# A graph layer on one core: TensorE's order inside a tile step

## Chip, core and metric

The kernel runs on one NeuronCore of a Trainium2 chip. The metric is the device time of one execution in microseconds; the kernel before was timed three times, with a median of 1980.95 us.

## What is computed

The input is x, 6250 nodes by 256 features, and 106250 edges (src, dst) that are sorted by dst, with two weights each. Cut to what matters:

```
xn  = layernorm(x)
low  = relu(segment_sum(edge_weight    * (xn @ W_low)[src],  dst))
high = relu(segment_sum(edge_weight_n2 * (xn @ W_high)[src], dst))
mlp  = relu(xn @ W_mlp)
att  = softmax(sigmoid([low@a_l, high@a_h, mlp@a_m]) @ att_vec / 3)
x1   = x + 3 * (att0*low + att1*high + att2*mlp) + mix(xn)
x2   = layernorm(x1)
w    = x2 @ wr + br
y    = gelu(x2 @ w1 + b1) @ w2 + b2        # FFN, 256 -> 1024 -> 256
out  = x1 + x2 + (y * w for the 3124 nodes with the largest w, else 0)
```

`mix` is a linear attention with an MLP over all nodes. The kernel multiplies by W_low and W_high after the sum over edges, which is the same.

## The kernel before

**First stage** (about 830 us of the profiled span). The nodes are handled in tiles of 128 rows, 49 in all. The edges are sorted by destination into 98 buckets of 64 nodes; the sorted records go to HBM by 448 indirect scatters on GpSimd (L648). Layer norm, `mix` and the third branch run beside it. None of it is touched.

**Second stage, the tile steps.** `pipeline` calls a function `stage(i, here, before1, before2, before3)` for i = 0 to 49 on each engine; the code is unrolled, every engine has its own list and they meet by semaphores alone. The flags say which tiles are in flight: in step i, `here` sums the edges of tile i, `before1` does the weight products of tile i-1, `before2` the FFN's first product of tile i-2, `before3` the FFN's second product of tile i-3.

The work of a step, by engine:

- **GpSimd** (L665) gathers the columns: one indirect DMA fetches 128 rows of xn (one edge on each partition) into a ring of 32 columns, 852 columns in all, about 8.7 a bucket. It waits for `col_free` ahead of each group of 8. **SyncE** (L554 to L564) watches gathers land in fours (`g_ready`) and hands columns back in groups of 8, when `sel_used` says that TensorE has used them; it does both in one queue, in order.
- **VectorE**: `post_b(i-2)` (L1203 to L1209: x2, its row sum with wr), `bucket(2i)`, `post_a(i-1)`, `bucket(2i+1)`. A `bucket` builds the one-hot weights of 2 x 5 columns (L1116 makes the mask, L1122 multiplies by the edge weights), signalled by `sel_ready`. `post_a` (L1164 to L1197) waits for `lh_ready`, makes two logit sums (L1167), exchanges two tanh with ScalarE, and forms x1 and the start of a Newton iteration.
- **TensorE** (matmuls at L1528, transposes at L1817 and L1827): a bucket is 10 products of 128 x 256 in fp32, accumulated in PSUM (bank 0 for the first bucket of a tile, bank 1 for the second). A step is: transposes of the two summed buckets (`before1`), bias row, transposes of x2, **weight products** (4), **first bucket**, `down` (8 products: FFN out), `up` (16 products of 128 x 128: FFN in), **second bucket**. An fp32 product is two matmul instructions in the profile.
- **ScalarE**: `sums(i)` copies the second bucket (L1443), the transposed sums (L1447), and makes the Relu copy of the weight products (L1452, `lh_ready`); `copy_x2t` (L1456); the copy of the first bucket (L1490, waits for `sel_used` 4i+2); `attention` (two tanh, L1460 and L1462); `newton` (L1468 to L1473); `scale_y` (L1481); the GELUs (L1438).

A bucket on TensorE waits twice for columns and twice for select weights:

```
pe.wait_ge(S("g_ready"), pe.snap(lo + VIS))
pe.wait_ge(S("sel_ready"), 2 * b + 1)
...
pe.wait_ge(S("g_ready"), pe.snap(rest + BOTH))
pe.wait_ge(S("sel_ready"), 2 * b + 2)
```

Once per step a chain crosses three engines: first bucket done, its copy and a tanh on ScalarE, `post_a` on VectorE, then VectorE's select of the second bucket, then TensorE's second bucket.

Of the kernel before, what the change touches and what calls it, by code (L numbers as in the profile page):

```python
# [43 lines left out]
def wait(eng, sem, value):  # L44

    if isinstance(value, int) and value <= 0:
        return
    eng.wait_ge(sem, value)


def build(nc, a, out):
# [47 lines left out]
    with ExitStack() as ctx:  # L99
        sems = {}  # L100

        def S(name):
            if name not in sems:
                sems[name] = ctx.enter_context(nc.semaphore(name))
            return sems[name]
# [121 lines left out]
        here = r2.take([P, NBUF, VIS, BK], BF16)  # L227
# [136 lines left out]
        bank = [ctx.enter_context(nc.psum_tensor(f"bank{i}", [P, 512], F32)) for i in range(8)]  # L364
# [39 lines left out]
        def bucket_word(eng, b):  # L404

            return eng.value_load(packed[0:1, b:b + 1], min_val=0, max_val=2 ** (2 * CBITS) - 1)

        def first_col(eng, word):
            return eng.snap(word % 2 ** CBITS, min_val=0, max_val=COLS - 1)

        def extra_cols(eng, word):
            return eng.snap((word // 2 ** CBITS) % 2 ** CBITS, min_val=0, max_val=COLS - 1)
# [883 lines left out]
        def _(act):  # L1296
# [138 lines left out]
            def gelu(i, part):  # L1435
                act.wait_ge(S("f1_psum"), 2 * i + part + 1)
                for f in range(part * KF // 2, (part + 1) * KF // 2):
                    act.activation(fh[:, f, :], bank[4 + part][:, (f % 4) * P:(f % 4 + 1) * P], ACT.Gelu_apprx_tanh,  # L1438
                                   bias=b1f[:, f:f + 1]).then_inc(S("fh_ready"), 1)

            def sums(i):
                act.wait_ge(S("sel_used"), 4 * i)
                act.activation(agg[:, 1, :], bank[1][:, 0:D], ACT.Copy).then_inc(S("agg_b"), 1)  # L1443
                act.wait_ge(S("at_psum"), i)

                for k in range(KD):
                    ins = act.activation(aggt[:, k, :, :].rearrange("p v (h n) -> p v h n", h=2),  # L1447
                                         bank[2][:, k * D:(k + 1) * D].rearrange("p (h v n) -> p v h n", h=2, v=2), ACT.Copy)
                ins.then_inc(S("aggt_ready"), 1)
                act.wait_ge(S("lh_psum"), i)  # L1450
                wait(act, S("lh_used"), i - 1)
                act.activation(lh[:, :], bank[3][:, :], ACT.Relu).then_inc(S("lh_ready"), 1)  # L1452

            def copy_x2t(a):
                act.wait_ge(S("xt_psum"), a + 1)
                act.activation(x2t[:, :, :].rearrange("p k n -> p (k n)"), bank[6][:, 0:D], ACT.Copy).then_inc(S("x2t_ready"), 1)  # L1456

            def attention(i):
                act.wait_ge(S("lg_ready"), i)
                act.activation(sg[:, 0, :], lg[:, :], ACT.Tanh, scale=0.5).then_inc(S("sig_tanh"), 1)  # L1460
                act.wait_ge(S("att_in"), i)
                act.activation(sg[:, 6, :], sg[:, 3, :], ACT.Tanh, bias=sg[:, 5, 0:1], scale=-1.0).then_inc(S("att_tanh"), 1)  # L1462
# [15 lines left out]
            def scale_y(a):  # L1478
                act.wait_ge(S("y_psum"), a + 1)
                act.wait_ge(S("w_ready"), a + 1)  # L1480
                act.activation(side[:, ds(a * D, D)], bank[7][:, 0:D], ACT.Copy, scale=wall[:, ds(a, 1)]).then_inc(S("y_ready"), 1)  # L1481

            def stage(i, here, before1, before2, before3):
                if before1:
                    sums(i)
                if before2:
                    copy_x2t(i - 2)
                if here:
                    act.wait_ge(S("sel_used"), 4 * i + 2)
                    act.activation(agg[:, 0, :], bank[0][:, 0:D], ACT.Copy).then_inc(S("agg_a"), 1)  # L1490
                if before1:
                    attention(i)
                if not here:

                    scale_y(i - 3)
                    gelu(i - 2, 0)
                    newton(i)
                    gelu(i - 2, 1)
                    return
                if before1:  # L1500
                    newton(i)
                if before3:
                    scale_y(i - 3)
                if before2:
                    gelu(i - 2, 0)
                    gelu(i - 2, 1)
# [19 lines left out]
        def _(pe):  # L1526
# [243 lines left out]
            def add_col(acc, weights, col, start, stop):  # L1770

                at = pe.snap((col % GR) * D)
                return mm(acc[:, 0:D], weights, rows[:, ds(at, D)], start, stop, skip_group_check=True)

            def bucket(b, acc):

                word = bucket_word(pe, b)
                lo = first_col(pe, word)
                more = extra_cols(pe, word)
                pe.wait_ge(S("g_ready"), pe.snap(lo + VIS))  # L1780
                pe.wait_ge(S("sel_ready"), 2 * b + 1)
                for j in range(VIS):
                    ins = add_col(acc, msel[:, 2 * b % NBUF, j, :], lo + j, j == 0, False)
                ins.then_inc(S("sel_used"), 1)
                with pe.If(more > 0):
                    done = extras_so_far(pe, b)
                    with pe.Fori(0, more) as e:
                        pe.wait_ge(S("g_ready"), pe.snap(lo + e + VIS + 1))
                        pe.wait_ge(S("sel_x_ready"), pe.snap(done + e + 1))
                        add_col(acc, msel_x[:, :], lo + e + VIS, False, False).then_inc(S("sel_x_used"), 1)  # L1790
                rest = pe.snap(lo + more)
                pe.wait_ge(S("g_ready"), pe.snap(rest + BOTH))
                pe.wait_ge(S("sel_ready"), 2 * b + 2)
                for j in range(VIS):
                    ins = add_col(acc, msel[:, (2 * b + 1) % NBUF, j, :], rest + VIS + j, False, j == VIS - 1)
                ins.then_inc(S("sel_used"), 1)
# [15 lines left out]
            def stage(i, here, before1, before2, before3):  # L1812
                if before1:
                    pe.wait_ge(S("agg_b"), i)
                    for k in range(KD):
                        for h in range(2):
                            ins = pe.transpose(bank[2][:, k * D + h * P:k * D + (h + 1) * P], agg[:, h, k * P:(k + 1) * P], ident[:, :])  # L1817
                    ins.then_inc(S("at_psum"), 1)
                if before3:

                    wait(pe, S("y_ready"), i - 3)
                    mm(bank[7][:, 0:D], ones_b[0:65, :], b2f3[0:65, :], True, False)
                    pe.wait_ge(S("fh_ready"), (i - 2) * KF)
                if before2:
                    pe.wait_ge(S("x2_ready"), i - 1)
                    for k in range(KD):
                        ins = pe.transpose(bank[6][:, k * P:(k + 1) * P], x2n[:, k * P:(k + 1) * P], ident[:, :])  # L1827
                    ins.then_inc(S("xt_psum"), 1)
                if before1:
                    if isinstance(i, int) and i == 1:  # L1830
                        pe.wait_ge(S("gnn_loaded"), 16 * 2)
                    pe.wait_ge(S("aggt_ready"), i)
                    wait(pe, S("lh_ready"), i - 1)
                    for v, w in enumerate((wlow, whigh)):
                        for k in range(KD):
                            ins = mm(bank[3][:, v * D:(v + 1) * D], aggt[:, k, v, :], w[:, k, :], k == 0, k == KD - 1)
                    ins.then_inc(S("lh_psum"), 1)
                if here:
                    wait(pe, S("agg_a"), i)
                    bucket(2 * i, bank[0])  # L1840
                if before3:
                    down(0, KF).then_inc(S("y_psum"), 1)
                if before2:
                    if isinstance(i, int) and i == 2:
                        pe.wait_ge(S("ffn_loaded"), 16 * 2)
                    pe.wait_ge(S("x2t_ready"), i - 1)
                    for part in range(2):
                        up(part).then_inc(S("f1_psum"), 1)
                if here:
                    wait(pe, S("agg_b"), i)  # L1850
                    bucket(2 * i + 1, bank[1])
# [64 lines left out]
```

## Time and profile before

| | us |
|---|---|
| timed, median of 3 runs | 1980.95 |
| timed, lowest and highest | 1979.86, 1987.71 |
| the profiled execution, its span (first to last instruction) | 2481.7 |
| TensorE matmuls busy | 1719.4 (69%) |
| GpSimd busy | 1371.7 (55%) |
| VectorE busy | 1229.1 (50%) |
| ScalarE busy | 924.8 (37%) |

The profile is of one execution, and for it only the span is given. It is 501 us longer than the median of the timed runs, so its parts can't be added up to the timed value without asking which of them belong to the profiled execution alone. PE is TensorE, PEld its weight loads, DVE VectorE, ACT ScalarE, POOL GpSimd, SP SyncE. In a row of a timeline the first number is the start, the second the length in us, then engine, line, operation, output<-input and count; the bracket holds the idle time before it and what ended it. "issue" is idle time for which the profile shows no wait.

### The profile page before, as it was taken

What the parts mean: (1) busy time and instruction counts of PE and PEld (TensorE: products, weight loads), DVE (VectorE), ACT (ScalarE), POOL (GpSimd) and SP (SyncE); (2) the same over time, 40 slices, a digit from 0 to 9 for tenths busy, and PEclk for the clock granted to TensorE, in tenths of its full rate; (3) what the DMA queues carried; (4) which work ended last, traced back from release to release, by engine and by line L of the source; (5) the groups of instructions that cost most, each with busy time, mean ns of one, the idle gap of its engine ahead of it and who ended that gap; (6) DMA issues with size and microseconds to landing.
All of it is one profiled execution on the core that took longest, in us unless ns stands there. A gap on an engine that the chain in (4) does not pass through costs nothing.

```text
span 2481.7 us, 30518 instructions
## 1 busy us (share of the span) xinstructions
PE 1719.4 (69%) x9109; PEld 1441.9 (58%) x9109; DVE 1229.1 (50%) x3164; ACT 924.8 (37%) x2641; POOL 1371.7 (55%) x1351
## 2 busy tenths in 40 slices
PE   4788884998865347776777677677577677667672
PEld 4566673887754335665665666566466566556562
DVE  8899995888761223432343333333333333333336
ACT  2677873777652112321222222222222222222223
POOL 3277675788776565545555455455455545554600
PEclk9899996999967667888887888788788788788886
DMA  3221211111100422222222222222222222222303
GB/s 90 72 63 54 80 33 30 46 54 46 46 5 5 133 85 72 78 69 75 71 74 71 68 73 75 65 72 75 68 73 75 75 69 71 81 71 68 85 9 104
DMA packets 102212, 162.99 MB, mean 66 GB/s; under 512 B 32190, under 2 KB 72762, under 8 KB 102040
## 3 DMA queue, kind: packets, MB, share of 16 engines
q0 software_dynamic: 55232, 113.59, 16.4%
q1 hardware_dynamic: 46808, 47.29, 6.0%
q8 instruction: 85, 1.39, 0.2%
q14 instruction: 87, 0.71, 0.1%
HBM read 139.76 MB, written 21.04 MB: 65 GB/s over the span
## 4 chain that ended last, share of the span: by engine, by line
PE 51%; issue 23%; DVE 10%; ACT 9%; another core or an unknown queue 5%; DMA 1%; SPq 1%; POOL 0%; DVEq 0%; ACTq 0%; POOLq 0%
PE bank L1528 49%; ACT side L1303 2%; PE bank L1817 1%; ACT base L1303 1%; ACT arena L1303 1%; DVE arena L811 1%; ACT arena L1447 1%; ACT arena L1443 1%; DVE arena L733 1%; ACT side L1519 1%; DVE arena L766 1%; ACT arena L1307 0%; PE bank L1602 0%; DVE arena L781 0%
## 5 line engine op out<-in xcount | busy, mean ns | idle before, releaser
L1528 PE MATMUL bank<-arena 128*128 128x128 f32 (+3 forms) x6320 | 1292.5, 359 | 508.2 <-issue 426.8
L1528 PEld LDWEIGHTS bank<-arena 128*128 128x128 f32 (+1 forms) x6320 | 1094.8, 205 | 683.8 <-issue 500.0
L665 POOL DMA_INDIRECT arena<-xn_rows,arena x852 | 825.5, 969 | 733.8 <-SPq L564 450.0
L648 POOL DMA_INDIRECT sorted_records<-arena x448 | 523.0, 1167 | 256.0 <-issue 139.3
L1167 DVE CUSTOM_DVE_ANT_0 arena<-arena 128x256 f32<-128x256 f32 x98 | 37.8, 423 | 414.9 <-ACT arena L1452 376.1
L1122 DVE TENSOR_TENSOR arena<-arena 128x640 f32<-128x640 bf16 (+1 forms) x204 | 164.2, 805 | 47.6 <-DVE arena L1116 17.7
L1172 DVE SCALAR_TENSOR_TENSOR att_prod<-sg,att_neg 128x9 f32<-128x9 f32 x49 | 8.5, 174 | 334.9 <-issue 300.8
L1490 ACT ACTIVATE arena<-bank 128x256 f32<-128x256 f32 x49 | 18.8, 383 | 355.5 <-remote 262.1
L1116 DVE SCALAR_TENSOR_TENSOR arena<-io,arena 128x320 bf16<-128x320 f32 (+1 forms) x204 | 97.8, 479 | 106.3 <-DVE wall L1209 43.5
L1528 PE MATMUL bank<-arena,base 128*128 128x128 f32 (+3 forms) x766 | 118.4, 287 | 16.7 <-ACT base L1307 8.3
L1438 ACT ACTIVATE arena<-bank,b1f 128x128 f32<-128x128 f32 x392 | 110.3, 372 | 33.5 <-PE bank L1528 28.1
L811 DVE TENSOR_TENSOR arena<-arena 128x1280 f32<-128x1280 bf16 x84 | 120.5, 1488 | 4.1 <-remote 1.7
L1528 PEld LDWEIGHTS bank<-arena,base 128*128 128x128 f32 (+2 forms) x766 | 110.2, 211 | 17.6 <-ACT base L1307 8.5
L1443 ACT ACTIVATE arena<-bank 128x256 f32<-128x256 f32 x49 | 18.8, 383 | 247.0 <-PE bank L1528 219.3
L1528 PE MATMUL bank<-side,arena 128*128 128x512 f32 x196 | 97.1, 619 | 0.3 <-issue 0.3
L1481 ACT ACTIVATE side<-bank,wall 128x256 f32<-128x256 f32 x49 | 23.1, 472 | 176.0 <-remote 165.3
L1303 ACT ACTIVATE base<-arena 128x128 f32<-128x128 f32 x280 | 84.7, 391 | 9.4 <-DVE arena L792 9.4
L1468 ACT ACTIVATE nr<-nri 128x1 f32<-128x1 f32 x49 | 9.9, 203 | 206.0 <-issue 159.8
L1303 ACT ACTIVATE arena<-arena 128x128 f32<-128x128 f32 x280 | 84.6, 397 | 0.0
L1303 ACT ACTIVATE side<-arena 128x128 f32<-128x128 f32 x280 | 84.6, 392 | 0.0
L1528 PE MATMUL bank<-arena,side 128*128 128x128 f32 x560 | 73.5, 282 | 12.0 <-issue 10.9
L1528 PEld LDWEIGHTS bank<-arena,side 128*128 128x128 f32 x560 | 68.0, 196 | 15.6 <-issue 14.1
(312 smaller groups left out, 1889.2 us busy)
## 6 DMA issues: line engine op xcount, KB each, us to landing
arena<-xn_rows,arena POOLq DMA_INDIRECT x852
sorted_records<-arena POOLq DMA_INDIRECT x448
arena<-in_x SPq DMA_DIRECT2D x12, 512.0 KB
xn_rows<-arena SPq DMA_DIRECT2D x12, 512.0 KB
x_plus_xn_rows<-arena SPq DMA_DIRECT2D x12, 512.0 KB
arena<-x_plus_xn_rows SPq DMA_DIRECT2D x12, 512.0 KB
arena<-xn_rows SPq DMA_DIRECT2D x12, 512.0 KB
out<-base SPq DMA_DIRECT2D x4, 1024.0 KB
```

Source lines behind the costliest of these rows:

```text
L648: pool.indirect_dma_start(rec_dram, bass.IndirectOffsetOnAxis(ap=idx[0:PR, par, u:u + 1], axis=0), stage_rec[0:PR, par, u * 8:(u + 1) * 8] ...
L665: pool.indirect_dma_start(gring[:, c % GR, :], None, xn_dram, bass.IndirectOffsetOnAxis(ap=rring[:, c, 3:4].bitcast(I32), axis=0)).then_in ...
L733: ins = dve.tensor_tensor(oh[:, t, :].rearrange("p j (h e) -> p j h e", e=2), twice[:, t, :].unsqueeze(2).to_broadcast([P, GS, NB // 2, 2] ...
L766: dve.tensor_tensor(prod4[:, :, :, 0:NB], oh[:, :, :].rearrange("p (s j) b -> p s j b", s=GROUPS), rankf[:, :].rearrange("p (s b) -> p s b ...
L811: dve.tensor_tensor(cellrec[:, t, :].rearrange("p t (f c) -> p t f c", f=4), cell[:, t, :].unsqueeze(2).to_broadcast([P, GS, 4, GC]), raw[ ...
L1116: return dve.scalar_tensor_tensor(out_, io64[:, :].unsqueeze(1).to_broadcast([P, n, BK]), float(BK * b), r[:, :, 0:1].to_broadcast([P, n, ...
L1122: return dve.tensor_tensor(out_, hots.unsqueeze(2).to_broadcast([P, n, 2, BK]), r[:, :, 1:3].unsqueeze(3).to_broadcast([P, n, 2, BK]), ALU ...
L1167: ins = dve.tensor_tensor_reduce(out=lg_prod[:, k, :], in0=lh[:, k * D:(k + 1) * D], in1=att_rows[:, k, :], scale=1.0, scalar=0.0, op0=ALU ...
L1303: ins = act.activation(quot[:, j, :], iota32[:, :], ACT.Abs, bias=p32[:, par, s * GS + j:s * GS + j + 1], scale=-1.0)
L1438: act.activation(fh[:, f, :], bank[4 + part][:, (f % 4) * P:(f % 4 + 1) * P], ACT.Gelu_apprx_tanh, bias=b1f[:, f:f + 1]).then_inc(S("fh_re ...
L1443: act.activation(agg[:, 1, :], bank[1][:, 0:D], ACT.Copy).then_inc(S("agg_b"), 1)
L1528: return pe.matmul(out_, lhsT, rhs, start=start, stop=stop, **kw)
```

## The change

TensorE runs the first bucket of a tile ahead of the weight products of the tile before, not behind them. ScalarE's Relu copy of those products moves from the end of `sums` to just ahead of `attention`, so that its copies keep TensorE's order: second bucket, transposed sums, x2, first bucket, Relu. The waits and semaphore counts are the same, and no instruction is added or taken away. In the last step (i = 49), where there is no bucket, ScalarE makes the x2 copy ahead of the Relu.

```
@@ scalar: sums(i)
                 ins.then_inc(S("aggt_ready"), 1)
+
+            def low_high(i):
                 act.wait_ge(S("lh_psum"), i)
                 wait(act, S("lh_used"), i - 1)
                 act.activation(lh[:, :], bank[3][:, :], ACT.Relu).then_inc(S("lh_ready"), 1)
@@ scalar: stage
                 if before1:
+                    low_high(i)
                     attention(i)
@@ tensor: stage
+                if here:
+                    wait(pe, S("agg_a"), i)
+                    bucket(2 * i, bank[0])
                 if before1:
...
                     ins.then_inc(S("lh_psum"), 1)
-                if here:
-                    wait(pe, S("agg_a"), i)
-                    bucket(2 * i, bank[0])
                 if before3:
                     down(0, KF).then_inc(S("y_psum"), 1)
```

## Rows read from the trace of the kernel before

**Rows 1.** The page: busy time of each engine, and the granted TensorE clock by slice.

```profile
PE 1719.4 (69%) x9109; PEld 1441.9 (58%) x9109; DVE 1229.1 (50%) x3164; ACT 924.8 (37%) x2641; POOL 1371.7 (55%) x1351
...
PEclk9899996999967667888887888788788788788886
```

**Rows 2.** Busy time by stretch of the span (start:end, length, then each engine).

```profile
core 0: us, PE busy (x) PEld busy (x) DVE busy (x) ACT busy (x) POOL busy (x), PEclk, DMA share, GB/s
...
832.00:2373.00 1541.00, 1059.66 (x4864) 897.34 (x4865) 542.86 (x1758) 378.46 (x1230) 825.19 (x852) 0.82 0.26 75
2373.00:2482.00 109.00, 50.66 (x245) 39.46 (x243) 59.13 (x158) 35.23 (x102) 0.19 (x1) 0.73 0.18 60
```

**Rows 3.** The list of waits, whole span: us in total, times, longest.

```profile
PE bank L1528 <- issue: 454.7, 347, 9.2
...
POOL arena L665 <- SPq L564: 450.0, 67, 13.1
```

**Rows 4.** One step in order of time, 1520 to 1528 us: TensorE and ScalarE.

```profile
1520.85 0.30 PE L1528 MATMUL bank<-arena 128*128 128x128 f32 x1 [1.83 <-issue]
...
1523.66 0.37 PE L1528 MATMUL bank<-arena 128*128 128x128 f32 x1 [2.52 <-issue]
...
1527.36 0.47 ACT L1481 ACTIVATE side<-bank,wall 128x256 f32<-128x256 f32 x1 [4.29 <-remote]
```

**Rows 5.** Stretches inside two steps; the number behind POOL's is the granted clock.

```profile
2368.70:2382.00 13.30, 13.30 (x76) 11.99 (x76) 5.43 (x25) 2.92 (x10) 2.98 (x4) 1.00 0.15 41
...
1521.00:1527.00 6.00, 0.89 (x3) 0.86 (x3) 3.46 (x8) 1.88 (x7) 3.10 (x3) 0.50 0.30 87
```

**Rows 6.** The last full step in order of time: ScalarE, TensorE and VectorE.

```profile
2366.85 0.38 ACT L1443 ACTIVATE arena<-bank 128x256 f32<-128x256 f32 x1 [4.83 <-PE bank L1528]
...
2367.89 0.38 PE L1827 MATMUL bank<-ident,arena 128*128 128x128 f32 x2
...
2368.69 13.34 PE L1528 MATMUL bank<-arena 128*128 128x256 f32 x76 [0.42 <-ACT arena L1447]
...
2370.72 0.60 ACT L1452 ACTIVATE arena<-bank 128x512 f32<-128x512 f32 x1 [2.08 <-PE bank L1528]
...
2371.35 0.43 DVE L1167 CUSTOM_DVE_ANT_0 arena<-arena 128x256 f32<-128x256 f32 x1 [9.04 <-ACT arena L1452]
...
2375.04 0.38 ACT L1490 ACTIVATE arena<-bank 128x256 f32<-128x256 f32 x1 [3.44 <-PE bank L1528]
...
2375.32 0.20 ACT L1460 ACTIVATE sg<-lg 128x3 f32<-128x3 f32 x1
...
2381.25 0.49 DVE L1116 SCALAR_TENSOR_TENSOR arena<-io,arena 128x320 bf16<-128x320 f32 x1 [0.69 <-issue]
...
2381.89 0.82 DVE L1122 TENSOR_TENSOR arena<-arena 128x640 f32<-128x640 bf16 x1
...
2383.02 2.20 PE L1528 MATMUL bank<-arena 128*128 x9 [1.00 <-DVE arena L1122]
```

**Rows 7.** GpSimd in order of time, where nothing holds it.

```profile
1507.20 0.95 POOL L665 DMA_INDIRECT arena<-xn_rows,arena  x1 [0.31 <-issue]
1508.45 0.95 POOL L665 DMA_INDIRECT arena<-xn_rows,arena  x1 [0.30 <-issue]
```

**Rows 8.** The page: GpSimd's gathers in groups.

```profile
L665 POOL DMA_INDIRECT arena<-xn_rows,arena x852 | 825.5, 969 | 733.8 <-SPq L564 450.0
```

**Rows 9.** ScalarE in order of time, 790 us: a stall ahead of the tile steps.

```profile
789.89 0.60 ACT L1326 ACTIVATE arena<-bank 128x512 f32<-128x512 f32 x1 [28.11 <-remote]
```

**Rows 10.** After the last step, in order of time: logit sums to tanh.

```profile
2409.57 0.43 DVE L1167 CUSTOM_DVE_ANT_0 arena<-arena 128x256 f32<-128x256 f32 x1 [7.91 <-ACT arena L1452]
...
2410.39 0.20 ACT L1460 ACTIVATE sg<-lg 128x3 f32<-128x3 f32 x1 [0.57 <-DVE lg L1167]
```

**Rows 11.** VectorE in order of time: `post_b` of a tile.

```profile
2400.02 0.41 DVE L1203 TENSOR_SCALAR arena<-arena,mv,nr 128x256 f32<-128x256 f32 x1
...
2401.26 0.21 DVE L1209 TENSOR_SCALAR wall<-nr,br 128x1 f32<-128x1 f32 x1
```

More of the change, by code:

```diff
@@ L1449, in sums, with low_high @@
                 ins.then_inc(S("aggt_ready"), 1)
+            def low_high(i):
                 act.wait_ge(S("lh_psum"), i)
@@ L1491, in stage @@
                 if before1:
+                    low_high(i)
                     attention(i)
@@ L1828, in stage @@
                     ins.then_inc(S("xt_psum"), 1)
+                if here:
+                    wait(pe, S("agg_a"), i)
+                    bucket(2 * i, bank[0])
                 if before1:
@@ L1837, in stage @@
                     ins.then_inc(S("lh_psum"), 1)
-                if here:
-                    wait(pe, S("agg_a"), i)
-                    bucket(2 * i, bank[0])
                 if before3:
```

## Prediction

> **What bounds the kernel now.** I read the totals first, then the stretches, then the list of waits, then single steps in order of time. The totals say TensorE 69% and GpSimd 55% [rows 1]; the stretches say that 1541 of the 2481.7 us lie between the first and the last of 852 column gathers on GpSimd, with TensorE busy for 1059.66 us of them [rows 2]. That is the stage of the 49 tile steps, and the only place where the diff does anything.
>
> The profiled execution is no picture of the timed one: 2481.7 us of span against a median of 1980.95, so 501 us are extra. The waits show where: TensorE idles 454.7 us for nothing that the profile names, in 347 pieces [rows 3]. In one step they look like this: single matmuls about 2.1 us apart, while ScalarE waits for a "remote" release [rows 4]. The granted clock is 0.50 there (the 1.2 GHz level) and 1.00 (2.4 GHz) in a step without such gaps [rows 5]. GpSimd's 450.0 us of waiting for SyncE's column credits [rows 3] are the same stalls seen from the producer: TensorE is late, the ring of 32 columns is full. I take these stalls as belonging to the profiled execution, because only their removal brings the span near the timed runs, and I cost the change on steps without them.
>
> The cleanest step is the last full one. Its 76 matmul instructions run in one piece of 13.34 us [rows 6], and the number fits: 8 for the weight products, 20 for the first bucket, 16 for the FFN's second product (`down`), 32 for its first (`up`). Counted from ScalarE's copy of the second bucket at 2366.85:
> - weight products start at 2368.69, 1.84 us later;
> - they are done at 2370.72 (the Relu copy starts), the first bucket at 2375.04 (its copy starts), 4.32 us later;
> - TensorE is through `down` and `up` at 2368.69 + 13.34 = 2382.03;
> - the second bucket starts only at 2383.02, after 1.00 us of waiting for VectorE's selection weights.
>
> So the way from "first bucket done" to "second bucket starts" is not TensorE's 7.0 us but 8.0 us through ScalarE's copy and tanh (2375.32), VectorE's attention work, and the select (2381.25 and 2381.89) [rows 6]. From a bucket's first matmul to its copy: 6.35 us for 28 instructions less 8 x 0.216 us (4.32 / 20), 4.62. The next step's origin is 2387.64; one step is 20.8 us, 49 are 1019.
>
> GpSimd has its own step. Gathers start 1.25 us apart when nothing holds them [rows 7], with 0.30 us idle between; by the group's mean of 969 ns [rows 8] plus 0.30 it is 1.27. 852 / 49 = 17.4 columns a step: 21.7 to 22.1 us, 1065 to 1082 in all. That is above 20.8. Which of the two holds in the timed runs? Take the profiled span, remove the gather stretch (1541) and one named stall of 28.1 us before it [rows 9], and 912.6 are left. The median leaves 1981 - 913 = 1068 us for the stage, 21.8 a step. GpSimd's pace gives 1065 to 1082, TensorE's chain 1019. So I hold that the timed kernel is bound by GpSimd's gather pace, with about 1 us a step of slack behind it. What lies outside the span isn't shown, nor are the smaller stalls of the first stage; they pull in opposite directions, so the fit is good to perhaps 30 us.
>
> On GpSimd's spans the Trainium skill (Perfetto Trace Analysis, section GPSIMD Engine Instruction) advises timing by start-to-start spacing and not by the reported duration. The trace agrees that the two differ, 1.25 against 0.969; by the duration alone the stage would be 852 x 0.969 = 826 us and TensorE's chain would bound instead.
>
> **The change part by part.** No instruction is added or removed; matmuls, copies, semaphores and waits are the same.
> - First bucket moved ahead of the weight products. Before, TensorE idles 0.42 us for ScalarE's transposed copy ahead of the weights [rows 6]. After, it can go on right behind the transposes of the FFN input, which end at 2367.89 + 0.38 = 2368.27 and are followed at issue pace: bucket at about 2368.2 instead of weights at 2368.69. Gain in TensorE's own order: 0.49 us a step. What it could meet instead is its own select (below) or its columns; where the gathers bind, waiting for columns at this place costs nothing, since the gathers run on.
> - Weight products moved behind the bucket. The Relu copy starts 6.35 us after the bucket's first matmul (28 instructions, the same count as now): 2374.55 instead of 2370.72.
> - ScalarE: copy of the first bucket at about 2372.82 instead of 2375.04, then the wait for the weights, then Relu, then the tanh. Queued behind that new wait are tanh, Newton steps, `scale_y` and the GELUs. VectorE waits for the Relu before the logit sums: before, these were long done while the bucket ran; now they are in the chain. From the Relu's start to VectorE 0.63 (2370.72 to 2371.35) [rows 6], from there to the tanh 0.82 (2409.57 to 2410.39) [rows 10]: tanh at 2376.00 instead of 2375.32, **0.68 us later**, although the bucket ended 2.2 earlier. Everything behind the tanh keeps its length, so the second bucket starts at 2383.70. TensorE is through with `up` at 2368.2 + 13.34 = 2381.54 and waits 2.2 us instead of 1.0.
> - GELUs of `up`: ScalarE's Newton steps follow VectorE's guess, so they slide by the same 0.68 and are read by `down` a step later, more than 10 us on: nothing.
> - SyncE's queue: it frees columns after each half bucket. Credits of the first bucket come 2.2 us earlier, those of the second 0.7 later. Worst case a full group of 8 columns (10 us) late once; best case nothing. The ring holds 32 columns and a bucket reads 10, so with GpSimd as the bound GpSimd never waits for it; nothing.
> - VectorE's select of the next first bucket is needed earlier: at 2387.64 + 0.68 + 1.35 = 2389.7 (the bucket starts 2368.20 - 2366.85 = 1.35 us into a step) instead of 3.6 us into it. By the rows: the second select's other half takes 1.4 us behind 2383.4 (one half is 1.46 us, 2381.25 to 2382.71) [rows 6], `post_b` 1.45 us (2400.02 to 2401.47) [rows 11], the next half select 0.7 + 1.46: 2388.4. It fits with 1.3 us; if it did not, what it is late would come on top.
>
> Sum for a step: chain 20.8 + 0.7 = 21.5 us, against GpSimd's 21.7 to 22.1. The later chain is still covered, by 0.2 to 0.6 us. What is uncovered is the end: once the last columns have landed, first bucket to second bucket takes 2383.70 - 2372.82 = 10.9 us instead of 8.0. That is +2.9 us, once. Forecast 1981 + 3 = **1984 us**.
>
> **The rivals.**
> - *Gathers don't bind, the chain does* (slower). The logit sums come into the chain from tanh to select; 49 x 0.68 = +33 us: 2014, or about half of it, 1998, where GpSimd binds in some steps and the chain in others. It decides as soon as the gathers' pace is below 21.5 us a step, that is below 1.235 us a column; 1.25 is only 1% above it. For it: 0.2 us of cover is thin, buckets differ in width, and the stage of 1068 us is known to 30. Against: 1019 is 49 us too short for the stage of before.
> - *TensorE's own order binds* (faster). If `down` and `up` (7.0 us at clock 1.00) take longer than the new chain from Relu to select, 2383.70 - 2374.55 = 9.15 us, the chain is hidden and 49 x 0.49 = 24 us come back: 1957. This needs a mean granted clock under 7.0 / 9.15 = 0.77 in that piece; the stretch had 0.82, but with the stalls in it [rows 2], and 1.00 in the clean step [rows 5].
> - *Nothing is reached*: each step's weights wait anyway for something else. That is the forecast's own time.
>
> The Trainium skill (Perfetto Trace Analysis, section Identifying the Most-Contended Engine) takes the engine with the highest occupancy as the bottleneck. By that rule it is TensorE, 69% against 55%, and the result would be the faster rival's 1957. The row of GpSimd's pace and the stage's length speak against it here.
>
> **How the numbers follow.** Covered by the gathers, 1984: 0.55. Chain, fully or in part, 1998 to 2014: 0.33. TensorE's own order, 1957 to 1971: 0.12. A measurement of this kernel tells about 0.5% (10 us) from no change, so these are also the chances of same, slower and faster. The range takes in the first two cases with 2 us above the full price, and goes down to 1968, which leaves most of the faster case out: 1968 to 2016.
>
> **What would show it.** In the profile of the changed kernel, in a step whose 76 matmuls run in one piece: the bucket's copy (now ahead of the Relu) about 6 us after the second bucket's copy; the Relu 1.7 us behind it; the tanh 1.4 us behind the Relu; TensorE's wait for the select 2.2 us instead of 1.0. Gathers still 1.25 us apart. The profiled span may move by tens of us with the stalls and decides nothing. I am wrong if GpSimd's free-running pace in the timed runs is not that of the profile, or if TensorE's clock without stalls stays low enough that its matmuls set the step.

## The result and the profile after

The changed kernel takes 2023.32 us (median of 4), the kernel before, run beside it, 1982.8: a ratio of 1.0194, 95% interval 1.0178 to 1.0209. It is about 40 us slower, outside the forecast's range by 7 us, and not the "no change" that I held likeliest.

The profiled execution of the changed kernel spans 2024.8 us; nothing of the 2.1 us gaps of [rows 4] is in it. The page of after:

```profile
span 2024.8 us, 30518 instructions
PE 1611.9 (80%) x9109; PEld 1364.5 (67%) x9109; DVE 1226.6 (61%) x3164; ACT 920.7 (45%) x2641; POOL 1388.0 (69%) x1351
...
PEclk9899999699999776899999999999999999999975
```

A second profile of the kernel before (the first experiment) spans 1979.9 us, as long as its timed runs. It, and not the one in front, is what after has to be held against. Its page:

```profile
span 1979.9 us, 30518 instructions
PE 1569.8 (79%) x9109; PEld 1325.9 (67%) x9109; DVE 1230.2 (62%) x3164; ACT 915.0 (46%) x2641; POOL 1395.7 (70%) x1351
```

Where the 44.9 us between the two spans lie can be read from one row a step, ScalarE's copy of the second bucket (L1443). Before, its first start is at 809.5 and its 49th at 1902.7, 1093.2 us apart; after, at 812.1 and 1946.7, 1134.6 apart. So 41.4 us of the 44.9 arise in the tile steps: 32 in the 45 steps of the middle, 5 in the two ahead of them, 4 in the last one (41.7 us instead of 37.9). Over 830 to 1880 us the granted clock is 0.94, against 0.98 in the second profile of before; in the page's tenths both look like 9. The waits of TensorE and GpSimd in the tile steps (830 to 1880 us), of after:

```profile
PE bank L1531 <- DVE arena L1122: 113.2, 55, 9.2
...
POOL arena L665 <- SPq L564: 42.9, 42, 3.5
...
PE bank L1531 <- SPq L554: 0.2, 1, 0.2
```

and of the second profile of before:

```profile
PE bank L1528 <- DVE arena L1122: 51.2, 46, 4.5
PE bank L1528 <- SPq L554: 47.4, 24, 4.9
...
POOL arena L665 <- SPq L564: 21.0, 69, 0.3
```

The bound has changed hands. Before, TensorE waits 47.4 us for landed columns (SyncE's L554) and GpSimd never for more than its usual 0.3 us: the gathers set the pace. After, TensorE never waits for columns, GpSimd now waits up to 3.5 us for freed ones, and TensorE's total wait for VectorE's select has more than doubled.

Two neighbouring steps of after in order of time, which answer to [rows 6]:

```profile
1259.01 0.38 ACT L1443 ACTIVATE arena<-bank 128x256 f32<-128x256 f32 x1 [3.41 <-PE bank L1531]
...
1260.66 13.33 PE L1531 MATMUL bank<-arena 128*128 x76 [0.22 <-issue]
...
1265.27 0.38 ACT L1492 ACTIVATE arena<-bank 128x256 f32<-128x256 f32 x1 [4.20 <-PE bank L1531]
1267.00 0.60 ACT L1454 ACTIVATE arena<-bank 128x512 f32<-128x512 f32 x1 [1.34 <-PE bank L1531]
...
1268.44 0.20 ACT L1462 ACTIVATE sg<-lg 128x3 f32<-128x3 f32 x1 [0.84 <-DVE lg L1167]
...
1276.16 6.27 PE L1531 MATMUL bank<-arena 128*128 x20 [2.17 <-DVE arena L1122]
...
1282.46 0.38 ACT L1443 ACTIVATE arena<-bank 128x256 f32<-128x256 f32 x1 [3.40 <-PE bank L1531]
...
1299.72 4.58 PE L1531 MATMUL bank<-arena 128*128 x20 [2.20 <-DVE arena L1122]
...
1304.34 0.38 ACT L1443 ACTIVATE arena<-bank 128x256 f32<-128x256 f32 x1 [1.74 <-PE bank L1531]
```

The 76 matmuls in one piece, the Relu 1.73 us behind the first bucket's copy, the tanh 1.44 behind it, the wait of 2.17: the order is as forecast, nearly to the tenth. What isn't is the second bucket: the same 20 instructions take 6.27 us in the first step and 4.58 in the second. The two stretches, columns as in [rows 2]:

```profile
1276.10:1282.40 6.30, 6.24 (x20) 4.89 (x20) 4.89 (x12) 2.93 (x11) 2.70 (x3) 0.73 0.19 55
1299.70:1304.30 4.60, 4.58 (x20) 3.72 (x20) 3.37 (x9) 2.87 (x11) 3.07 (x3) 1.00 0.30 89
```

The granted clock is 0.73 in the one, so more than half of it ran at 1.2 GHz, and 1.00 (2.4 GHz) in the other. The steps are accordingly of two lengths: by the starts of L1443, of the 45 steps in the middle 11 take about 21.8 us and 34 about 23.5, a mean of 23.1. Before they range from 20.8 to 28 with a mean of 22.4, since TensorE waits for columns in bursts.

So the theory at this point, **clock**: the new order alone gives a step of 21.8 us, which the gathers would still cover; but TensorE's wait of 2.2 us ahead of the second bucket lets the clock fall in three steps of four, that costs 1.7 us each, and 23.1 is above the gathers' pace. Its rivals: **chain** (the longer way to the select is the whole loss), and **ring** (columns are freed later, so GpSimd is held up).

### The profile page after: what moved, and what is told of

Same layout as the page of the kernel before. It is cut to its first block, busy times and chain, and to the rows that moved or that the text cites. A ratio compares the mean times of both kernels' runs of the same rounds, so it can differ in the third digit from the quotient of the medians.

```text
span 2024.8 us, 30518 instructions
## 1 busy us (share of the span) xinstructions
PE 1611.9 (80%) x9109; PEld 1364.5 (67%) x9109; DVE 1226.6 (61%) x3164; ACT 920.7 (45%) x2641; POOL 1388.0 (69%) x1351
## 4 chain that ended last, share of the span: by engine, by line
PE 29%; DVE 18%; issue 6%; ACT 4%; POOL 3%; DVEq 2%; DMA 0%; ACTq 0%; SPq 0%; POOLq 0%
PE bank L1531 28%; DVE arena L1122 2%; POOL arena L665 2%; DVE arena L1116 2%; DVE arena L1167 2%; ACT arena L1454 1%; PE bank L1820 1%; DVE arena L1186 1%; DVE arena L1189 1%; DVE ybuf L1187 1%; DVEq L406 1%; DVE st L1190 1%; ACT side L1522 1%; ACT sg L1464 1%; ACT arena L1443 1%
## 5 line engine op out<-in xcount | busy, mean ns | idle before, releaser
L1531 PE MATMUL bank<-arena 128*128 128x256 f32 (+3 forms) x6320 | 1188.8, 347 | 156.1 <-DVE arena L1122 129.4
L1531 PEld LDWEIGHTS bank<-arena 128*128 128x128 f32 (+1 forms) x6320 | 1017.4, 193 | 305.5 <-issue 173.9
L665 POOL DMA_INDIRECT arena<-xn_rows,arena x852 | 842.4, 989 | 300.9 <-issue 255.5
L1122 DVE TENSOR_TENSOR arena<-arena 128x640 f32<-128x640 bf16 (+1 forms) x204 | 164.1, 804 | 31.3 <-DVE arena L1116 3.1
L1438 ACT ACTIVATE arena<-bank,b1f 128x128 f32<-128x128 f32 x392 | 106.1, 385 | 5.0 <-PE bank L1531 5.0
L1443 ACT ACTIVATE arena<-bank 128x256 f32<-128x256 f32 x49 | 18.8, 383 | 170.3 <-PE bank L1531 170.3
L766 DVE TENSOR_TENSOR arena<-arena 128x2940 f16<-128x2940 bf16 x28 | 47.3, 1688 | 48.5 <-ACT arena L1313 48.3
L1531 PE MATMUL bank<-arena,side 128*128 128x128 f32 x560 | 67.4, 275 | 0.0
L1531 PE MATMUL bank<-arena,ones_f 98*128 98x294 f32 (+2 forms) x74 | 27.2, 451 | 48.6 <-DVE arena L829 32.1
```

The source lines that it names most:

```text
L665: pool.indirect_dma_start(gring[:, c % GR, :], None, xn_dram, bass.IndirectOffsetOnAxis(ap=rring[:, c, 3:4].bitcast(I32), axis=0)).then_in ...
L766: dve.tensor_tensor(prod4[:, :, :, 0:NB], oh[:, :, :].rearrange("p (s j) b -> p s j b", s=GROUPS), rankf[:, :].rearrange("p (s b) -> p s b ...
L1122: return dve.tensor_tensor(out_, hots.unsqueeze(2).to_broadcast([P, n, 2, BK]), r[:, :, 1:3].unsqueeze(3).to_broadcast([P, n, 2, BK]), ALU ...
L1531: return pe.matmul(out_, lhsT, rhs, start=start, stop=stop, **kw)
```

## The experiments

**1. Before, again.** No edit.

> The kernel before, unchanged, for a second profile. Theory A (the first profile's 2.1 us gaps are a disturbance of that one execution): span near 1980 us, steps without those gaps, and TensorE waiting about 1 us a step for the select of the second bucket. Theory B (the gaps belong to this order of work): span near 2480 again. Both: time within 0.5% of 1983.

Time 1981.61, span 1979.9 us. Theory A holds: the gaps of [rows 4] belonged to that one execution. TensorE's wait for the select is 1.0 to 1.25 us in nearly every step, and in none of the 45 steps of the middle is the second bucket slow behind it. One of its steps:

```profile
1237.28 13.34 PE L1528 MATMUL bank<-arena 128*128 128x256 f32 x76 [0.42 <-ACT arena L1447]
...
1251.62 4.58 PE L1528 MATMUL bank<-arena 128*128 x20 [1.01 <-DVE arena L1122]
```

In a few steps the second bucket stops once more halfway, for columns. Behind such a stop of 1.81 us its other 10 instructions still take 2.42 us; behind one of 2.74 us they take 3.37, so the kernel before shows the same fall of the clock where it waits long enough:

```profile
963.56 2.42 PE L1528 MATMUL bank<-arena 128*128 x10 [1.81 <-SPq L554]
...
1343.64 3.37 PE L1528 MATMUL bank<-arena 128*128 x10 [2.74 <-SPq L554]
```

**2. Filling the wait.** The changed kernel with five products that nobody reads:

```
                     for part in range(2):
                         up(part).then_inc(S("f1_psum"), 1)
+                    for _ in range(5):
+                        mm(bank[6][:, D:2 * D], w1f[:, 0, 0:P], w1f[:, 1, 0:D], True, True)
                 if here:
                     wait(pe, S("agg_b"), i)
```

> The changed kernel, with 5 more fp32 products of 128 x 256 (2.16 us) on TensorE between `up` and the second bucket, into half a PSUM bank that nobody reads; they fill the wait for the select. Theory clock (the wait of 2.2 us makes the granted clock fall in the second bucket, which costs 1.7 us in most steps): all steps of 21.8 us, 49 x 0.8 x 1.7 = 60 us back at most, or as much as the gathers' pace leaves, 1965 to 1990. Theory chain alone (the longer chain is the whole loss): no change within 0.5% or slower, 2018 to 2035.

1967.42 us against 1984.0: ratio 0.9913 (0.9897 to 0.993). More work on TensorE takes 56 us from the changed kernel and makes it faster than the kernel before. The bucket, products, FFN, filling and second bucket run in one piece, and the steps are 21.8 us, 41 of the 45 in the middle:

```profile
1260.26 20.09 PE L1531 MATMUL bank<-arena 128*128 x106 [0.22 <-DVE arena L1122]
...
1280.39 0.39 ACT L1443 ACTIVATE arena<-bank 128x256 f32<-128x256 f32 x1 [1.70 <-PE bank L1531]
```

The select is ready no sooner: from the first bucket's copy to the start of the second bucket it is 10.9 us with and without the filling. So the longer chain alone is refuted as the cause. What has changed is that TensorE doesn't idle ahead of the second bucket, and that in all 45 steps of the middle this bucket's 20 instructions take 4.58 us.

**3. How much filling.** The same loop with 2 products, and with 9.

> As after_filled, with 2 filling products (0.86 us), so that 1.3 us of the wait stay idle, nearer to the 1.0 us of the kernel before, whose clock seldom fell. Theory clock (what costs is the length of the idle time ahead of the second bucket, not the wait itself): low clock in few steps, steps of 21.8 us, 1965 to 1985. Rival (any idle time there drops the clock, or only back-to-back work keeps it): 2000 to 2025.

> As after_filled, with 9 filling products (3.89 us), 1.7 us more than the wait, so that the second bucket starts 1.7 us late in every step, at the high clock. Theory (the step is the chain of 21.8 us plus whatever delays the second bucket): steps of 23.5 us all at clock 1.00, 2030 to 2050, as slow as the low clock made it. Rival (the filling itself speeds something up, clock or not): under 2000.

With 2 products: 1968.71 us, ratio 0.992 (0.9902 to 0.9939). TensorE still waits 1.3 us in most steps and 1.46 at most, yet the second bucket takes 4.58 us in all 45 steps of the middle:

```profile
1270.54 4.58 PE L1531 MATMUL bank<-arena 128*128 x20 [1.31 <-DVE arena L1122]
...
1490.74 4.58 PE L1531 MATMUL bank<-arena 128*128 x20 [1.46 <-DVE arena L1122]
```

With 9 products: 2026.07 us, ratio 1.0204 (1.018 to 1.0229), a little better than the 2030 expected. The stage runs at a granted clock of 1.00, and loses as much as the unfilled kernel does by its clock. The row of 830 to 1880 us, columns as in [rows 2], of this kernel:

```profile
830.00:1880.00 1050.00, 1012.44 (x5427) 889.82 (x5428) 512.36 (x1673) 356.28 (x1173) 774.61 (x786) 1.00 0.34 99
```

Its steps are 23.2 us long, not 23.5: the second bucket starts 1.5 us later than in the unfilled kernel. So 1.5 us of delay in each step and 1.7 us of slow matmuls in three of four come to nearly the same time; the loss can be had either way, by delay or by clock.

**4. The two halves of the change.** TensorE's order alone (ScalarE's Relu stays in `sums`):

```
@@ tensor: stage
+                if here:
+                    wait(pe, S("agg_a"), i)
+                    bucket(2 * i, bank[0])
                 if before1:
```

> TensorE's half of the change alone: first bucket ahead of the weight products, ScalarE's Relu copy still in `sums`, so that it stands ahead of the copies of x2 and of the first bucket. The first tanh still waits for Relu and logit sums (1.45 us behind the Relu's start), which covers the two copies. Theory (TensorE's order alone makes the loss, ScalarE's moved copy nothing): 2018 to 2030. Rival (the wait for x2's copy, now behind the weights, delays something): slower than 2030.

2023.17 us, ratio 1.0191 (1.0174 to 1.0208): the whole loss, and ScalarE's move adds nothing to it. The wait ahead of the second bucket is again 2.2 us, and that bucket is slow in 35 of the 45 steps of the middle. ScalarE's order alone:

```
                 if before1:
+                    low_high(i)
                     attention(i)
```

> ScalarE's half of the change alone: TensorE's order as before (weight products, then first bucket), but the Relu copy behind the copy of the first bucket, right ahead of the tanh. Theory (what costs is that Relu and logit sums stand between first bucket and tanh, and that the longer wait lets the clock fall): tanh 1.4 us later against the first bucket than before, TensorE waits 2.4 us, step 22.2 at full clock and 1.7 more where the second bucket runs at the low level, 2030 to 2050. Rival (TensorE's order is the cause, this half is harmless): 1974 to 1994.

2056.9 us, ratio 1.0368 (1.0345 to 1.039), worse than the whole change and 7 us beyond what I expected. Here the first bucket ends late and the Relu still stands behind it:

```profile
1467.90 0.38 ACT L1492 ACTIVATE arena<-bank 128x256 f32<-128x256 f32 x1 [6.12 <-PE bank L1531]
1468.18 0.59 ACT L1454 ACTIVATE arena<-bank 128x512 f32<-128x512 f32 x1
...
1469.66 0.20 ACT L1462 ACTIVATE sg<-lg 128x3 f32<-128x3 f32 x1 [0.90 <-DVE lg L1167]
```

From the bucket's copy to the tanh it is 1.76 us instead of 0.28 [rows 6]. TensorE waits longer still, and in all 45 steps of the middle, each of 23.9 us, the second bucket is slow (6.0 to 6.3 us):

```profile
1477.49 6.09 PE L1531 MATMUL bank<-arena 128*128 x20 [2.60 <-DVE arena L1122]
```

What the two halves have in common is that Relu and logit sums stand between the first bucket and the tanh. That is where the loss comes from, and not from TensorE's order as such. Here a part of it is the chain's own: without its slow matmuls the step would be about 22.4 us.

**5. Are the gathers the bound of before?** First, 2 filling products in the kernel before, where the wait is 1.0 us.

> The kernel before with 2 more fp32 products of 128 x 256 (0.86 us) on TensorE between `up` and the second bucket. Theory (before is paced by the gathers, and its 1 us waits seldom lower the clock): no change within 0.5%, 1974 to 1994. Rival (the clock costs before something too): up to 15 us faster, 1968.

1984.15 us, ratio 1.0 (0.9988 to 1.0011): filling has no virtue of its own where the clock doesn't fall. Then gathers of 64 rows in both kernels (sums over the other 64 rows are left out; those partitions are cleared once):

```
-                    gring[:, c % GR, :], None, xn_dram,
-                    bass.IndirectOffsetOnAxis(ap=rring[:, c, 3:4].bitcast(I32), axis=0))
+                    gring[0:64, c % GR, :], None, xn_dram,
+                    bass.IndirectOffsetOnAxis(ap=rring[0:64, c, 3:4].bitcast(I32), axis=0))
```

> The kernel before, but each gather fetches 64 rows, not 128 (partitions 64 to 127 of the ring are cleared once and stay zero, about 10 us of GpSimd), to make GpSimd's pace faster; what TensorE, VectorE and ScalarE do is the same. Theory gathers (1.30 us a column set the stage of before, 1111 us): if a gather of 64 rows takes under 1.15 us, the chain of 20.8 us a step takes over, stage 1020 to 1040 us, time 1905 to 1930. Rival (the chain sets it anyway): 1985 to 2000.

> The changed kernel with gathers of 64 rows as in before_half_rows. Theory (TensorE's chain at 21.8 us and the clock set its step): no gain from faster gathers, 2015 to 2035, so 5% slower than before_half_rows. Rival (its loss comes from the ring: GpSimd waits for columns 25 times): with cheap gathers the loss shrinks, under 1950.

The lever is weak: half the rows shorten a gather only from 998 to 936 ns. The row of before_half_rows, 830 to 1880 us:

```profile
L668 POOL DMA_INDIRECT arena<-xn_rows,arena x817 | 764.8, 936 | 248.9 <-issue 226.1 <-SPq L564 22.8
```

Even so the kernel before drops to 1934.29 us (0.9747, 0.9724 to 0.977), by 51 us, and the changed one stays at 2030.42 (1.0242, 1.0219 to 1.0264), 5% apart. The 1905 to 1930 us expected of the kernel before were for gathers under 1.15 us from start to start. They came out at 1.24, and clearing the ring lets the first one start 8 us later (785.6 us), so 1934 is no surprise. The stretch from the first gather to the last shrinks from 1110.7 to 1056.3 us. That shows both bounds: the gathers hold the kernel before, and don't hold the changed one. It also disposes of the ring: with cheaper gathers GpSimd waits longer for freed columns in the changed kernel, 80.8 us in 830 to 1880 us instead of 42.9, which is the sign of a producer that is held by its consumer:

```profile
POOL arena L668 <- SPq L564: 80.8, 51, 4.4
```

Cheap gathers and filling together were not run; how much the chain of 21.8 us costs by itself, once the gathers no longer cover it, stays open.

**6. The tanh ahead of the bucket's copy.** If the way from first bucket to select is what fails, it can be shortened on ScalarE instead:

```
+                if before1:
+                    attention(i)
                 if here:
                     act.wait_ge(S("sel_used"), 4 * i + 2)
                     act.activation(agg[:, 0, :], bank[0][:, 0:D], ACT.Copy).then_inc(S("agg_a"), 1)
-                if before1:
-                    attention(i)
```

> The kernel before, with ScalarE's two tanh ahead of its copy of the first bucket. The logit sums are ready while the first bucket still runs, so VectorE's attention work starts about 3 us earlier and the select is ready before TensorE is through with `up`. Theory chain (first bucket done, tanh, VectorE, select sets the step of before): the wait of 1 us and any low clock behind it go, 20 to 60 us faster, 1925 to 1963. Theory gathers (GpSimd's 1.25 us a column sets the step of before): no change within 0.5%, 1973 to 1993, and GpSimd's gathers without waits.

1969.23 us, ratio 0.9922 (0.9905 to 0.9938): 15 us, between the two expectations, below what the chain theory wanted and above the 0.5% of the gather theory. TensorE's wait for the select all but goes, and its wait for columns takes the place, 830 to 1880 us:

```profile
PE bank L1528 <- SPq L554: 87.7, 40, 6.0
...
PE bank L1528 <- DVE arena L1122: 4.2, 4, 1.1
```

GpSimd is never held for more than 0.3 us, so the gathers bind here too. This kernel, after_filled and after_fill2 beat both kernels of the comparison, by 0.8 to 0.9% against before, and lie together.

## Why the prediction was wrong

- *The gap in the profile.* Right: the 501 us were a disturbance of that execution. But I took only the 28.1 us of [rows 9] off the first stage. The clean profile has its first gather at 777.6 us, not at 832, so 54 us were extra there. The part behind the last gather was 110 us in that profile and is 92 in the clean one. I subtracted both as if they were in the timed runs, so my remainder of 1068 us for the stage was 43 us too small; it is 1111. So the fit that I counted as evidence for the gathers (1068 against their 1065 to 1082) was a coincidence: the stage and the gathers' pace were both taken too short, by 3 to 4%.
- *The gathers bind.* Right, shown by experiment 5 and by the waits. Their pace is 1.30 us a column in the clean profile (1110.7 us for 852), where I had 1.25 to 1.27. But the pace isn't a constant of the kernel, as my 1984 took it to be: in after_filled, the new order at full clock, it is 1.28, and the time is 1967. So even with the clock put right my "no change" would have been 17 us off.
- *The new chain of 21.5 us.* Mis-sized by 0.3: the first bucket starts 1.65 us into a step (1259.01 to 1260.66), not 1.35. The rest is as put: tanh 0.28 before and 3.17 behind the first bucket's copy after, first to second bucket 10.9 us (1265.27 to 1276.16), wait 2.2. At 21.8 us it is just about level with the gathers: in after_filled 41 of 45 steps are that long, their mean is 22.0, and GpSimd is never held for more than 0.3 us.
- **The step that failed: the clock.** I costed every step at a granted clock of 1.00, because the cleanest step had it [rows 5], and wrote "Everything behind the tanh keeps its length". I had put TensorE's wait at 2.2 us instead of 1.0 and asked only what it adds to the chain, not what the engine does after it. Nor did I read the second bucket's length anywhere: the 2387.64 that I called the next step's origin is 2383.02 plus the first bucket's 4.62 and stands in no row. In that trace the bucket behind 2383.02 stops again and again for its select, and its copy starts at 2405.07. The clean profile does have steps of 20.8 us, so what I had assumed without reading holds for before, and fails for after. The second bucket's 20 instructions take 6.27 instead of 4.58 us in three of four steps: 34 x 1.7 / 45 = 1.3 us a step, 21.8 to 23.1. I did look at the clock, but only as a way for TensorE's own order to win.
- *The slower rival* had the right side, at 2014, but by the wrong mechanism: it needed gathers faster than the chain. Chain and clock together pass the gathers' pace; the chain alone doesn't (after_filled), and the clock alone was not run. Its price should have had 1.7 us in a good part of the steps on top, and the range would have reached past 2023.
- *The end, +2.9 us*: the way is as put, 10.9 us from first to second bucket in the last step instead of 8.0. Its price isn't seen by itself: that step is 3.8 us longer, with slow matmuls in both kernels, but only 0.9 us longer in after_filled. Behind the last L1443 the two kernels differ by 0.9 us.
- *The rule of highest occupancy* would have named TensorE and a gain. Clean, before has 79% on TensorE against 70% on GpSimd, and GpSimd binds.

The Trainium skill has a warning that I had not drawn on (TensorE: Matmul & The Clock Gate, section HAM oscillation): a wait that returns between bursts of matmuls can bring the clock down anew each time. The runs here agree: the wait is one of 2.2 us for VectorE's select, and 34 of 45 second buckets behind it take 6.27 us instead of 4.58.

## What to carry to other kernels

A move that lengthens an engine's wait can have two prices: the wait, and, on TensorE, matmuls behind it at a lower clock (here 1.7 us behind a wait of 2.2, in three steps of four). Where a forecast says "now waits 2.2 us instead of 1.0", cost the work behind the wait at both clock levels. And before a profile is used for sums, hold its span against the timed runs; here they differed by a quarter, its cleanest rows held (the 76 matmuls in 13.34 us, the wait of 1.0), and what was left by subtraction was 43 us off.

## What the runs showed of the hardware

How the second bucket ran behind waits of different length, always behind 76 or 80 matmuls at a granted clock of 1.00 (45 steps in the middle of each run; a bucket is slow where its 20 instructions take over 6 us, waits inside it left out):

| kernel | wait ahead of the second bucket, us | slow second buckets | its length, us |
|---|---|---|---|
| after_fill2 | 1.3, at most 1.46 | 0 of 45 | 4.58 |
| after | 2.2 (2.16 to 2.38) | 34 of 45 | 6.27, or 4.58 |
| tensor_half | 2.2 | 35 of 45 | 6.27, or 4.58 |
| scalar_half | 2.4 to 2.7 | 45 of 45 | 6.0 to 6.3 |

The kernel with 2 unused products a step is 55 us faster than the one without (1968.71 against 2023.32), though it does more work: they shorten the wait from 2.2 to 1.46 us, and the 20 instructions behind it then run at 4.58 us throughout.

A gather's length on GpSimd varies with its surroundings, 998 ns on average in the kernel before and 977 in after_filled, with single ones of 1.27 us and more beside VectorE's select:

```profile
L665 POOL DMA_INDIRECT arena<-xn_rows,arena x807 | 805.6, 998 | 245.9 <-issue 224.8 <-SPq L564 21.0
```

```profile
L665 POOL DMA_INDIRECT arena<-xn_rows,arena x816 | 797.3, 977 | 248.7 <-issue 228.6 <-SPq L564 20.1
```

21 ns x 852 is 18 us, as much as the filled kernel's lead over before. In the kernel before, about 240 of the 852 gathers overlap a multiplication of the select (L1122) and take 1.10 us on average, the others 0.96; in after_filled about 200 overlap and take 1.02. That the select is the reason was not tried and stays open.
